# A graph layer on one core: three parts of 38, 5 and 6 row tiles, and two rows of each opening chunk normalized on GpSimd

## What is computed

```python
xn  = layernorm(x)
gnn = segment_sum(xn[src] * edge_weight[:, None], dst) @ weight
k, v normalized by head;  dots = k^T v;  mix = (q @ dots) / n @ Wout + bout
x   = x + gnn + mix
y   = layernorm(x)
logits = y @ gate_w + gate_b                  # 16 experts
e1, e2 = two best experts;  p = softmax of their logits
moe = sum over the two of p * (relu(y @ w1[e] + b1[e]) @ w2[e] + b2[e])
out = x + layernorm(y + moe) * gamma + beta
```

## Time and profile before

| | us |
|---|---|
| median of 3 runs | 1497.17 |
| lowest and highest run | 1494.88, 1503.07 |
| the profiled execution | 1489.54 |
| its span, first to last instruction | 1487.7 |

### The profile page before, as it was taken

The page is one execution under the profiler, slowest core; times in us unless marked ns, Lnnn a source line. Parts: engine busy times, 40 slices in busy tenths (PEclk is TensorE's granted clock), DMA queues, the critical chain, the costliest instruction groups (busy, mean ns, idle before and its releaser), DMA issues. The chain is left out here.

```text
span 1487.7 us, 21903 instructions
## 1 busy us (share of the span) xinstructions
PE 1023.5 (69%) x6498; PEld 761.3 (51%) x6498; DVE 651.1 (44%) x2406; ACT 406.0 (27%) x1085; POOL 1007.7 (68%) x1094
## 2 busy tenths in 40 slices
PE   0099999997764889744199641896674997558880
PEld 0055555554542778522077520775553886447870
DVE  7545454443457422323223332225144233528776
ACT  4144343332121324201033210332221332214330
POOL 4477777777755767777777777777767774176734
PEclk9999999999977899956589865999886999889995
DMA  9676656733321998633489534895855985289883
GB/s 336 173 239 206 205 163 196 235 105 104 99 81 68 318 358 279 214 105 103 160 268 362 179 103 138 279 329 194 301 206 189 329 303 188 82 296 346 268 300 117
DMA packets 153597, 317.09 MB, mean 213 GB/s; under 512 B 24608, under 2 KB 97568, under 8 KB 153344
## 3 DMA queue, kind: packets, MB, share of 16 engines
q0 software_dynamic: 49296, 134.68, 28.9%
q1 hardware_dynamic: 64320, 142.25, 27.3%
q10 hardware_dynamic: 39856, 38.67, 7.7%
HBM read 251.15 MB, written 64.36 MB: 212 GB/s over the span
## 5 line engine op out<-in xcount | busy, mean ns | idle before, releaser
L873 POOL DMA_INDIRECT ring<-normed_rows,src_sb x831 | 799.4, 962 | 326.0 <-issue 286.5
L1528 PE MATMUL ps<-ring,S 128*32 128x256 f32 x1680 | 133.8, 462 | 233.0 <-DMA ring<-normed_rows,src_sb 148.2
L1664 PE MATMUL ps<-room 128*128 128x128 f32 x1872 | 240.1, 284 | 17.8 <-DMA room<-in_w1b 17.0
L1664 PEld LDWEIGHTS ps<-room 128*128 128x128 f32 x1872 | 228.4, 199 | 22.9 <-issue 20.6
L1677 PE MATMUL ps<-room 128*128 128x256 f32 x936 | 225.4, 384 | 9.2 <-issue 9.2
L1528 PEld LDWEIGHTS ps<-ring,S 128*32 128x32 f32 x1680 | 58.8, 126 | 281.4 <-issue 252.6
L1461 DVE TENSOR_TENSOR desk<-ps,room 128x256 f32<-128x256 f32 x121 | 51.2, 424 | 330.6 <-PE ps L1677 324.7
L1677 PEld LDWEIGHTS ps<-room 128*128 128x128 f32 x936 | 171.6, 194 | 30.9 <-issue 12.0
L1555 PE MATMUL ps<-room,tT 128*128 128x512 f32 x392 | 177.4, 595 | 0.0
L983 ACT ACTIVATE room<-ps,room 128x128 f32<-128x128 f32 x468 | 133.4, 368 | 122.7 <-PE ps L1664 122.7
L843 POOL DMA_INDIRECT rows_by_slot<-X,slot_i x98 | 96.1, 981 | 78.9 <-DVEq L1353 47.8
(11 more groups left out here) (226 smaller groups left out, 1176.5 us busy)
## 6 DMA issues: line engine op xcount, KB each, us to landing
room<-in_w2b SPq DMA_DIRECT2D x87, 640.0 KB, 6.6
room<-in_w1b SPq DMA_DIRECT2D x87, 514.0 KB, 5.7
room<-rows_by_slot SPq DMA_DIRECT2D x121, 128.0 KB
results_by_slot<-desk ACTq DMA_DIRECT2D x121, 128.0 KB
rows_by_slot<-desk ACTq DMA_DIRECT2D x6, 2432.0 KB
ring<-normed_rows,src_sb POOLq DMA_INDIRECT x831
normed_rows<-X SPq DMA_DIRECT2D x7, 896.0 KB, 7.7
result<-ring SPq DMA_DIRECT2D x49, 128.0 KB, 4.0
```

Of the source, the lines that this page charges most:

```text
L873: pool.indirect_dma_start(out=ring[:, b % 2 * BT + m, :], out_offset=None, in_=table, in_offset=bass.IndirectOffsetOnAxis(ap=src_sb[:, b * ...
L1528: mm = pe.matmul(acc[w * W:(w + 1) * W, :], S[b % 2][:, m, :], ring[:, b % 2 * BT + m, :], start=(t == 0), stop=(t == GT - 1), skip_group_ ...
L1664: mm = pe.matmul(hps[g % 2][:, f * TS:(f + 1) * TS], w1_sb[g % WB][:, k * F + f * P:k * F + (f + 1) * P], xgT[g % 2][:, k, :], start=(k == ...
```

## The change

- The first part now ends at row tile 38 (before: 40); a second part of 5 row tiles ends at 43, a third of 6 at 49. The routings end at 8, 16, 24, 32, 38, 43 and 49. Everything derived from `PT` and `SUB` follows: buffers, lists, the planner's order.
- In the opening the two rows of a chunk that VectorE normalized are normalized by GpSimd; table store and TensorE wait for GpSimd's count instead of VectorE's.
- ScalarE takes the square root of chunk c + 1 ahead of normalizing chunk c.
- The edge weights and the weight matrix `wkv` are issued behind the table's stores instead of ahead of them, with a semaphore of their own, on which VectorE waits at the point where it used to wait for all three constants.

```diff
+POOL_ROWS = CH - ACT_ROWS
-PT = (0, 40, NT)
-SUB = (0, 8, 16, 24, 32, 36, 40, NT)
+PT = (0, 38, 43, NT)
+SUB = (0, 8, 16, 24, 32, 38, 43, NT)
...
-        CONSTS = [(ew[:, :], edge_w), (src_sb[:, :], src), (wkv_sb, wkv)]
+        CONSTS = [(src_sb[:, :], src)]
+        EDGE_CONSTS = [(ew[:, :], edge_w), (wkv_sb, wkv)]
...
             for c in range(NC):
                 sp.wait_ge(normed, ACT_ROWS * (c + 1))
-                sp.wait_ge(dve_normed, c + 1)
+                sp.wait_ge(pool_normed, POOL_ROWS * (c + 1))
                 sp.dma_start(rows_of(table, c * CH, CH), X2[:, c * CH:(c + 1) * CH, :]).then_inc(table_out, 16)
+            for o, i in EDGE_CONSTS:
+                sp.dma_start(o, i).then_inc(edge_consts_in, 16)
...
+            for c in range(NC):
+                pool.wait_ge(rstd_done, c + 1)
+                for q in range(c * CH + ACT_ROWS, (c + 1) * CH):
+                    pool.tensor_scalar(X2[:, q, :], X2[:, q, :], rstd[:, q:q + 1], nmr[:, q:q + 1],
+                                       ALU.mult, ALU.add).then_inc(pool_normed, 1)
+
             pool.wait_ge(table_out, 16 * NC)
...
-            for c in range(NC):
+
+            def root_chunk(c):
                 act.wait_ge(stats_done, c + 1)
                 act.activation(std0[:, c * CH:(c + 1) * CH], mv[:, c * CH:(c + 1) * CH, 1], ACT.Sqrt,
                                bias=eps_t[:]).then_inc(std_done, 1)
+            root_chunk(0)
+            for c in range(NC):
+                if c + 1 < NC:
+                    root_chunk(c + 1)
                 act.wait_ge(rstd_done, c + 1)
...
-                for q in range(c * CH + ACT_ROWS, (c + 1) * CH):
-                    ins = dve.tensor_scalar(X2[:, q, :], X2[:, q, :], rstd[:, q:q + 1], nmr[:, q:q + 1],
-                                            ALU.mult, ALU.add)
-                ins.then_inc(dve_normed, 1)
...
-            dve.wait_ge(consts_in, 16 * len(CONSTS))
+            dve.wait_ge(edge_consts_in, 16 * len(EDGE_CONSTS))
...
-            pe.wait_ge(dve_normed, NC)
+            pe.wait_ge(pool_normed, POOL_ROWS * NC)
```

More of the change, by code:

```diff
@@ L527, in gps_layer @@
         tables_in = sem("tables_in")
+        edge_consts_in = sem("edge_consts_in")
         later_in = sem("later_in")
@@ L533, in gps_layer @@
         normed = sem("normed")
-        dve_normed = sem("dve_normed")
+        pool_normed = sem("pool_normed")
         table_out = sem("table_out")
```

## The result

The changed kernel takes 1544.65 us in the median of 4 runs beside 1498.6 for the kernel before, ratio 1.030 [1.026, 1.035]; a second measurement gave 1.0345 [1.032, 1.038]. It is **45 to 52 us slower**. The forecast was 12 us slower (1509, range to 1524): the direction held, the size did not. The profiled execution has a span of 1542.8 us, where the forecast's sum was 1499.8. Of the four runs of one later kernel (after_latefins) one took 2750.6 us; it is left out of that kernel's number.

What follows compares the result with a forecast made beforehand. GpSimd's gathers pace the body, VectorE the opening. Opening and body sum to 0 (-5.6 + 7.6 - 2); tail 1291 + 178 + 30.8 ends at 1499.8, 12.1 us later: 1509 us, range 1487 to 1524.

Steps and rivals of the forecast that it cites:

- Opening: Before the first gather: VectorE's index work and the table finish earlier; gain 6.6 to 4.8 us, 5.6 taken.
- slows VectorE: Rival in the opening: GpSimd's operation takes over 1.5 us or slows VectorE, losing the 5.6; +18, 1515 us, chance 0.06.
- Body, visits, loads, bytes: Last gather stays at 1249 within 6 us; 130 visits, 94 weight loads; 59.7 MB moved in the tail.
- The end behind the last product: Tail's close: 37.5 us before, six fetches fewer take off 7.7, a larger last group adds about 1: 30.8 us.
- Slots at 1291: Tail: the last routing's slots come after 42 us instead of 44.8, with one gate fewer and narrower rows.
- three layers 1: Tail, beside the last routing: TensorE gets through three layers 1 and one layer 2 before VectorE finishes the slots.
- Pace of 41 visits, 178 us: Tail behind the slots: 170 us by bytes at 350 GB/s, 188 at before's pace, 178 taken; last product at 1469.
- TensorE's floor: Rival in the tail: loads hide behind products, 158 us for the visits, from 378 GB/s on; 1489 us, chance 0.28.
- Before's pace stays: Rival in the tail: 4.48 us a visit, 188 us instead of 178; +22, 1519 us, chance 0.13.
- that rival's 14: Rival in the body: TensorE falls behind in slots 58 to 66, GpSimd loses 14 us, not 6; 1517 us, chance 0.08.
- The rate of the page: Tail's transfer rate: the page's 358 GB/s gives 167 us by bytes, 435 gives 137; the prediction sided with 358.

Runs made afterwards that it cites:

- after_latefins: Changed kernel with the closing steps of the first row tiles queued on all engines only behind the last routing's list; 1.0327 of the kernel before (+49 us).
- after_held: Changed kernel with part two's first visit held behind the last mix and the last routing's slots; 1.0307 of the kernel before (+46 us).
- after_all: Changed kernel without spare list places, second boundary run without a drain, part two's first visit and closing steps behind the last routing; 1.0174 of before (+26 us).
- thin loads: Changed kernel with every weight load of parts two and three cut to a quarter, those rows wrong; 1.0206 of before (+31 us). With all order repairs: 0.9994.
- after_rep: Changed kernel timed once more, unaltered, beside later kernels on the same chip; 1.0345 of the kernel before (+52 us).
- after_cap_flow: Changed kernel without spare list places, loads issued ahead over the second boundary and the visit pipeline kept running there; 1.0236 of the kernel before (+35 us).
- two parts and the order repaired: New opening and routings in parts of 38 and 11 row tiles, part two's first visit and closing steps behind the last routing; 1.0012 of before (+2 us).

## Why the prediction was right and wrong

**Opening: right in the sum, in part by luck.** Forecast -5.6 at the first gather, measured -5.67, and 6.4 us in time (3 to 10). The flag, with the first gather 2.04 us behind it as before, was to gain 6.6 and gained 5.68; the forecast's 5.6 was a middle between flag and table, taken because the moved constants land beside the first gathers. Most of the missing 0.9 was lost on VectorE instead. GpSimd's operation takes 0.56 us, as forecast, in twelve of fourteen cases. But the last two, 1.02 and 0.74, run beside the end of `scale_chunk` and the index work, and there four operations of VectorE take 0.65 us longer together than before. The fourteen on GpSimd (ns: min/median/max), then VectorE's timeline:

```profile
L829 POOL TENSOR_SCALAR X<-X,rstd,nmr x14: 557/559/1024, 16.1 to 36.1; 128x256 f32<-128x256 f32 x14
...
34.77 0.49 DVE L1059 CAST desk<-desk 128x280 f32<-128x280 int32 x1 [0.19 <-issue]
...
36.47 0.42 DVE L1065 TENSOR_SCALAR desk<-desk 128x70 f32<-128x70 f32 x1
```

Before, the first took 0.30 us and the second 0.22:

```profile
42.36 0.22 DVE L1053 TENSOR_SCALAR desk<-desk 128x70 f32<-128x70 f32 x1
```

The rival that GpSimd "slows VectorE" was thus real, but at 0.65 us and not at the 5.6 it needed. The Trainium skill's page GPSIMD Engine Reference, section 4.1, would have the operation some two times VectorE's time for two inputs; this one, with one tile and two scalars a partition, takes 1.5 times VectorE's (1.10 for two, 0.74 in the earlier trace rows).

**Body, visits, loads, bytes: right.** Last gather 1250.14 for 1249; twelve traces with this opening and these routings lie between 1244.9 and 1254.4. 130 visits, 94 loads. The forecast's 59.7 MB behind the slots are 59.77 in the trace. The end behind the last product is 27.6 for 30.8.

**Slots at 1291: wrong by 9.7.** The step took 44.8 us of the earlier trace rows, less one gate, and let TensorE do "three layers 1" beside the routing. It saw that a visit of part two stands in slot 69; it did not ask what that visit waits for. TensorE's order has it ahead of the last mix, and its rows come 11.77 us late, most of it because SyncE stands at the left-out run of part one. With that visit moved back the slots were written at 1289.46 and the scatter started at 1292.64 (after_held), so the 42 us of the step were right. What sets the scatter then is GpSimd's twenty fetches ahead of it, a limit that the step did not weigh.

**Pace of 41 visits, 178 us: wrong, the largest term.** It has two errors.

First, the rate. The step took 350 GB/s from the best 62 us of the tail and then half of what before stood over it. Row, which the same paragraph uses for its bytes, has the mean, 313. 59.7 MB at 313 are 191 us, the last product ends at 1482, and the sum gives 25 us slower than before. after_all, in which the orders are repaired, measures +26, with 306 GB/s (62.48 MB in 204 us). The two rates agree; that the two times do is partly luck, for after_all's term is 204 us and not 191, its last product ends at 1492.9, and a shorter end and a fast trace of the kernel before make up for it. The step should have taken the mean of a whole comparable stretch.

```profile
DMA packets 30985, 62.48 MB, mean 306 GB/s; under 512 B 4496, under 2 KB 20752, under 8 KB 30961
```

Whether it is the bytes or the time that each load takes to land that paces these visits was not separated; thin loads take away both.

Second, the holes. The working had 41 visits as one stream. There are three pieces: a start that VectorE's closing steps crowd (51.8 us for 30), a boundary at which SyncE, ScalarE and TensorE each finish the old part before they begin the new one (20.5 for 3.7), and two stretches that mostly the loads pace. No term stood for a part's end, though the earlier trace rows show the kernel before waiting at its own; there the last routing had to be waited for anyway. The boundary's 16.8 us over a visit's 3.73 are: the left-out run 5.3, loads not issued ahead 3.4, the pipeline's drain at the end of a run 3.7, and 4.4 that stay; each is a difference of single traces, which scatter by 1 to 2 us there (20.4 to 22.1 where the boundary is unaltered). With both terms, 191 for the bytes and 16.8 for the boundary, the working gives 208 of the 214.5 us. All repairs of order together are worth 26 us of the 52.

**The rivals.** TensorE's floor was given 0.28 and decided from 378 GB/s held over the stretch: no run came near. "Before's pace stays" (+22) was nearest, and its reason, a late row that holds the next weights in SyncE's one order, is part of what stands at the boundary (six result stores from 1390.04 on, ahead of the load at 1402.02). The sum of that rival with a late start would still have fallen short: holes were in none of them. TensorE did not fall behind in the body of this trace: GpSimd's three waits for it from batch 60 on were 2.9, 1.8 and 2.8 us, 7.5 together where 6 was taken. In after_rep they were 4.1, 3.9 and 3.7, and 12.5 in all, near that rival's 14: the wait is not fixed from one execution to the next.

**The rate of the page.** The Trainium skill, DMA: Bandwidth & Descriptors, section Where 436 GB/s comes from, gives 358 GB/s as binding between memory and the on-chip buffer. Here the mean of a tail stays well under it, 279 in the changed kernel and 295 to 306 in four others, so it was no help for the term. Yet of the forty slices of 38 us on the page of the kernel with all orders repaired, one lies above it, 377:

```profile
GB/s 318 200 235 236 179 228 204 180 202 104 98 56 222 347 248 328 111 104 137 233 348 242 102 134 231 316 247 136 222 258 232 271 240 128 341 305 377 322 228 128
```

So 358 was no ceiling for this core, and neither figure is the pace of a kernel whose loads come in bursts.

## What to carry to other kernels

Price an added stage at the mean rate of a whole comparable stretch, not at the best window in it, and give its boundary a term of its own: for each in-order stream, what has to end before the next stage's first load, copy or store may start. A visit that is placed early to fill a gap stands in front of everything behind it on its engine, so ask what it waits for. And where two limits lie close, run the pair of repairs and not only each alone: here the orders were worth 26 us by the timed runs, thin loads 15 to 21, both together 46 to 53.

## What the runs showed of the hardware that was not expected

A wait of TensorE can cost twice, for behind it the granted clock may be at the lower of its two levels. In the kernel whose boundary is closed (after_cap_flow), sixteen products of layer 1 take 3.75 us behind the 3.07 us wait quoted above and 1.95 in the next visit; by window the granted clock there is 0.50 and then 1.00 (1.2 and 2.4 GHz). The transfers of a window are those that start in it, so in so short a one their share can pass 1:

```profile
1401.60:1405.20 3.60, 3.56 (x17) 3.59 (x18) 0.76 (x4) 0.00 (x0) 0.00 (x0) 0.50 1.05 414
1407.50:1409.30 1.80, 1.80 (x18) 1.80 (x17) 1.41 (x5) 0.55 (x2) 1.50 (x2) 1.00 0.87 207
```

Between slots and last product the changed kernel and the thin one run the same 1086 products, in 175.87 busy us at a mean granted clock of 0.91 and in 166.71 at 0.95: by this estimate up to 9 of the 24 us between them are clock. The forecast had no term for it.

Beside one another GpSimd and VectorE were slower in some operations and not in others. In all fifteen traces with the new opening GpSimd's last two operations take 1.02 and 0.74 us, and VectorE's four beside them 0.30, 0.49, 0.57 and 0.41 to 0.44 us, where the two traces with the old opening have 0.17, 0.30, 0.45 and 0.22. Beside GpSimd's other pairs VectorE's statistics take 2.38 us as before, and GpSimd 0.56. What the slow ones share was not tried.

From the slots to the last product the transfers' mean rate is much the same in four kernels with full loads: 301 GB/s before, 295 with the opening alone, 306 with all orders repaired, 300 with two parts and the order repaired, at a busy share of 0.87 to 0.89. The changed kernel with its holes has 279 at 0.83. The landing of the first weight table moves more: 7.3 us in the median of the repaired kernel's stretch, 5.0 in that of before, 3.2 when cut to a quarter.
